# The last batch's late norm steps handed to the next stage, and two sets of semaphores, in a twelve-stage decoder kernel

## The reference

```python
x = _layernorm(x + _L0_attn_ref(x, ...), axis=-1)
x = _layernorm(x + _L0_xattn_ref(ctx_1024, x, ...), axis=-1)
x = _layernorm(x + _L0_ffn_ref(x, ...), axis=-1)
x = _layernorm(x + _L1_attn_ref(x, ...), axis=-1)
...
x = _layernorm(x + _L3_ffn_ref(x, ...), axis=-1)

def _layernorm(x, axis=-1, eps=1e-05):
    m = jnp.mean(x, axis=axis, keepdims=True)
    v = jnp.var(x, axis=axis, keepdims=True)
    return (x - m) / jnp.sqrt(v + eps)
```

## Time and profile before

| what | us |
|---|---|
| median of 3 runs (lowest, highest) | 3104.22 (3101.42, 3107.92) |
| the profiled execution | 3098.92 |
| its span | 3097.2 |

### The profile page before, as it was taken

How to read it: one execution, slowest core, us unless ns; L and a number is a source line. 1 busy time by engine, 2 the same in 40 slices (tenths; PEclk the granted TensorE clock), 3 DMA queues, 4 the chain that set the end, 5 groups by cost and what they waited for, 6 DMA issues and landing times. The chain is left out here.

```text
span 3097.2 us, 43720 instructions
## 1 busy us (share of the span) xinstructions
PE 2643.9 (85%) x15420; PEld 1245.2 (40%) x15420; DVE 2037.3 (66%) x5373; ACT 1334.3 (43%) x2298; POOL 996.5 (32%) x1254
## 2 busy tenths in 40 slices
PE   6997869988775988898988999988764999798998
PEld 1333324423322433454563444444332333344555
DVE  6885851269996746676784666657576887673444
ACT  2775642275642642221213433435641577463221
POOL 3212100078896101333443555563045111210000
PEclk9998979988977989999999999998875899899999
DMA  5322300000002500122230000003100321320000
GB/s 127 64 36 43 77 21 1 0 1 0 1 0 49 115 10 19 28 52 57 52 73 20 1 1 1 1 4 61 21 0 11 53 48 27 81 60 1 4 4 8
DMA packets 52134, 95.66 MB, mean 31 GB/s; under 512 B 14966, under 2 KB 36266, under 8 KB 46462
## 3 DMA queue, kind: packets, MB, share of 16 engines
q1 hardware_dynamic: 50620, 90.39, 13.9%
q10 hardware_dynamic: 1296, 2.47, 0.3%
HBM read 46.20 MB, written 1.38 MB: 15 GB/s over the span
## 5 line engine op out<-in xcount | busy, mean ns | idle before, releaser
L1970 POOL TENSOR_TENSOR mamba_dbu<-mamba_du,mamba_b 128x512 f32<-128x512 f32 x128 | 244.4, 1909 | 41.9 <-DVE stream L2003 12.1
L2003 DVE TENSOR_TENSOR_SCAN stream<-mamba_da,mamba_dbu 128x512 f32<-128x512 f32 x128 | 215.2, 1682 | 18.3 <-issue 13.1
L1714 PE MATMUL ps<-stream,weights 128*128 128x512 f32 x256 | 154.3, 714 | 57.8 <-DVE stream L2013 42.7
L2858 DVE CUSTOM_DVE_ANT_0 ps<-ps,bconst 128x512 f32<-128x512 f32 (+3 forms) x256 | 119.4, 512 | 116.0 <-PE ps L2685 116.0
L664 DVE TENSOR_REDUCE L3a_negmax<-ps 128x1 f32<-128x512 f32 x256 | 160.7, 683 | 25.2 <-PE ps L368 25.1
L664 DVE TENSOR_REDUCE L0a_negmax<-ps 128x1 f32<-128x512 f32 x256 | 160.6, 683 | 23.4 <-PE ps L368 23.3
L485 ACT ACTIVATE L0a_probs<-ps 128x512 f32<-128x512 f32 x256 | 141.7, 600 | 60.3 <-PE ps L387 59.4
L485 ACT ACTIVATE L3a_probs<-ps 128x512 f32<-128x512 f32 x256 | 141.9, 601 | 56.6 <-PE ps L387 55.7
L2921 ACT ACTIVATE skv_probs<-ps 128x1024 f32<-128x1024 f32 (+3 forms) x128 | 90.2, 704 | 175.5 <-PE ps L2710 175.5
L165 POOL TENSOR_SCALAR vareps<-mv 128x4 f32<-128x4 f32 x24 | 8.8, 367 | 487.5 <-DVE mv L1444 487.3
L190 PE MATMUL ps<-stream,xT 128*64 128x512 f32 x512 | 126.9, 612 | 14.4 <-DVE moa_v L2461 7.2
(11 more groups left out here) (668 smaller groups left out, 6499.3 us busy)
## 6 DMA issues: line engine op xcount, KB each, us to landing
moa_masks<-picked SPq DMA_DIRECT2D x32, 512.0 KB, 6.6
stream<-stream SPq DMA_DIRECT2D x28, 192.0 KB
stream<-gate_up_down_in SPq DMA_DIRECT2D x16, 272.0 KB, 3.4
stream<-value_output_in SPq DMA_DIRECT2D x16, 256.0 KB, 3.6
pre<-gates SPq DMA_DIRECT2D x32, 128.0 KB
stream<-ffn_in SPq DMA_DIRECT2D x16, 180.5 KB, 2.9
pre<-pre SPq DMA_DIRECT2D x40, 64.0 KB
L0a_qs<-L0a_qs SPq DMA_DIRECT2D x16, 128.0 KB
```

What stands on the lines that cost most here:

```text
L1714: pe.matmul(ps[:, SUM_BANK + j, :], k.ident, hc[:, (J * i + j) % RING, :], start=n == 0, stop=n == N - 1).then_inc(s["summed"], 1)
L1970: pool.tensor_tensor(dbu[:, m % RING, :], du[:, b % 2, j, :], bsb[:, i % B_RING, :], ALU.mult).then_inc(s["dbu_ready"], 1)
L2003: dve.tensor_tensor_scan(out=hs[:, m % RING, :], data0=da[:, m % RING, :], data1=dbu[:, m % RING, :], initial=0.0, op0=ALU.mult, op1=ALU.a ...
L2858: last = dve.tensor_tensor_reduce(ps[:, bank + a, 0:n], ps[:, bank + a, 0:n], later[:, SEQ - n:], -1.0, 3e38, ALU.add, ALU.min, negmax[:, ...
```

## The change

Two parts. First, `phase` draws from two pools of 50 semaphores in turn. The block's own barrier stays, SP's clearing comes behind it, and the second barrier is gone (also behind the last stage).

Second, in every stage but the last, batch 3's steps behind the statistics are left out (`left_over`), and each stage but the first does them for its forerunner, on six semaphores of their own (`k.late`) that count stages and are never cleared. POOL's two instructions (`late_deviation`) and DVE's four (`late_rescale`) stand at or near the head of their queues; PE's four turns (`late_turn`) and ACT's copy (`late_keep`) stand some steps later, in a PSUM bank that is free then; `late_known` is a wait ahead of the first reader. With mamba as the forerunner DVE rescales where ACT did, and POOL's two instructions for the offset (1975, 1976) fall away for batch 3. In the cross attentions the clearing of `v` moves to the very head of DVE's queue, ahead of `late_rescale`.

```diff
 def phase(k, *names):
...
-    assert len(names) <= len(k.pool), (len(names), len(k.pool))
-    s = dict(zip(names, k.pool))
+    pool = k.pools[k.stage % 2]
+    assert len(names) <= len(pool), (len(names), len(pool))
+    s = dict(zip(names, pool))
     with nc.Block() as block:
         yield block, s
-    used = k.pool[:len(names)]
-    nc.sync.sem_clear(range(used[0].num, used[-1].num + 1))
-    nc.all_engine_barrier()
+    nc.sync.sem_clear(range(pool[0].num, pool[len(names) - 1].num + 1))
+    k.stage += 1
...
+LATE = ("var", "eps", "rstd", "x", "xT", "sb")
+
+
+def left_over(k, b):
+    return b == BATCH - 1 and k.stage < STAGES - 1
+
+
+def late_deviation(k, pool):
+    if k.stage:
+        pool.wait_ge(k.late["var"], k.stage)
+        pool.tensor_scalar(k.vareps[:, :], k.mv[:, :, 1], EPS, None, ALU.add).then_inc(k.late["eps"], 1)
+        pool.wait_ge(k.late["eps"], k.stage)
+        pool.tensor_tensor(k.rstd[:, :], k.vareps[:, :], k.minus_half, ALU.pow).then_inc(k.late["rstd"], 1)
+        pool.wait_ge(k.late["rstd"], k.stage)
+
+
+def late_rescale(k, dve):
+    if k.stage:
+        dve.wait_ge(k.late["rstd"], k.stage)
+        for t in range(NT):
+            last = dve.tensor_scalar(k.xs[:, BATCH - 1, t, :], k.resid[:, t, :], k.mv[:, t, 0:1], k.rstd[:, t:t + 1],
+                                     ALU.subtract, ALU.mult)
+        last.then_inc(k.late["x"], 1)
+        dve.wait_ge(k.late["x"], k.stage)
+
+
+def late_turn(k, pe, bank):
+    if k.stage:
+        pe.wait_ge(k.late["x"], k.stage)
+        for t in range(NT):
+            last = pe.transpose(k.ps[:, bank, t * P:(t + 1) * P], k.xs[:, BATCH - 1, t, :], k.ident)
+        last.then_inc(k.late["xT"], 1)
+
+
+def late_keep(k, act, bank):
+    if k.stage:
+        act.wait_ge(k.late["xT"], k.stage)
+        act.copy(k.xTs[:, BATCH - 1, :], k.ps[:, bank, :]).then_inc(k.late["sb"], 1)
+
+
+def late_known(k, eng, sem="sb"):
+    if k.stage:
+        eng.wait_ge(k.late[sem], k.stage)
...
                 def turn_x(b):
+                    if left_over(k, b):
+                        return
                     pe.wait_ge(s["x_ready"], b + 1)
...
-                    last.then_inc(s["var_ready"], 1)
+                    last.then_inc(k.late["var"] if left_over(k, b) else s["var_ready"], 1)
...
+                    if J == LATE_AT:
+                        late_turn(k, pe, Z_BANK)
+                    if J == LATE_AT + 2:
+                        late_known(k, pe)
...
             @block.gpsimd
             def _(pool):
                 chain = Chain(pool, s["pool_chain"])
+                late_deviation(k, pool)
...
+                pad_v()
+                late_rescale(k, dve)
                 dec = out_t[:, :].rearrange("p (t d) -> p t d", t=NT)
...
                 for J in range(FIRST, LAST):
-                    if batch_at(J, PAD_AT) == 0:
-                        pad_v()
...
                 scale_logits(0)
+                late_rescale(k, dve)
                 route(0)
```

More of the change, by code:

```diff
@@ L28 @@
 PIECES = 16
+STAGES = 12
 SMALL = ["wq", "wk", "wv", "wo", "bv", "bo", "bq", "bk"]
@@ L760, in _ @@
                             add_out(batch_at(J, Y_AT + 1))
-                        if batch_at(J, Y_AT + 2) is not None and a == 1:
-                            b = batch_at(J, Y_AT + 2)
+                        b = batch_at(J, Y_AT + 2)
+                        if b is not None and a == 1 and not left_over(k, b):
                             scaled(k.xs[:, b], b + 1).then_inc(s["x_ready"], 1)
@@ L1171, in _ @@
                             rstd(2 * batch_at(J, Y_AT) + 1)
-                        if batch_at(J, Y_AT + 1) is not None:
-                            rstd(2 * batch_at(J, Y_AT + 1) + 2)
-                    elif batch_at(J, Y_AT + 1) is not None:
+                        b = batch_at(J, Y_AT + 1)
+                        if b is not None and not left_over(k, b):
+                            rstd(2 * b + 2)
+                    elif batch_at(J, Y_AT + 1) is not None and not left_over(k, batch_at(J, Y_AT + 1)):
                         rstd(batch_at(J, Y_AT + 1) + 1)
@@ L1258, in stats @@
                         last = dve.bn_aggr(k.mv[:, t, :], k.stats[:, t, :])
-                    last.then_inc(s["var_ready"], 1)
+                    return last
                 def scaled(out, n):
@@ L1279, in half_stats, with aggregate @@
                     chain(last)
-                def aggregate():
+                def aggregate(b):
                     for t in range(NT):
                         last = dve.bn_aggr(k.mv[:, t, :], k.stats[:, t, :])
-                    last.then_inc(s["var_ready"], 1)
+                    last.then_inc(k.late["var"] if left_over(k, b) else s["var_ready"], 1)
+                pad_v()
+                late_rescale(k, dve)
                 dec = out_t[:, :].rearrange("p (t d) -> p t d", t=NT)
@@ L1340, in _ @@
                             else:
-                                aggregate()
-                        if batch_at(J, XT_AT) is not None and a == 1:
-                            b = batch_at(J, XT_AT)
+                                aggregate(batch_at(J, Y_AT + 1))
+                        b = batch_at(J, XT_AT)
+                        if b is not None and a == 1 and not left_over(k, b):
                             scaled(k.xs[:, b], 2 * b + 2 if scrambled else b + 1).then_inc(s["x_ready"], 1)
@@ L1435, in residual, with statistics @@
         chain(ins)
-    statistics(k, dve, chain, s)
-def statistics(k, dve, chain, s):
+    statistics(k, dve, chain, s, b)
+def statistics(k, dve, chain, s, b):
     for t in range(NT):
@@ L3116, in _ @@
                         experts(batch(J, 1), 6, 8)
+                    if J == 0:
+                        late_turn(k, pe, D_BANK)
+                    if J == 2:
+                        late_known(k, pe)
                     if batch(J, 4) is not None:
@@ L3577, in build @@
         k.gates = nc.dram_tensor("gates", (BATCH, 8, SEQ), F32).ap()
-        k.pool = [ctx.enter_context(nc.semaphore(f"stage_{i}")) for i in range(50)]
+        k.pools = [[ctx.enter_context(nc.semaphore(f"{n}_{i}")) for i in range(50)] for n in ("even", "odd")]
+        k.late = {n: ctx.enter_context(nc.semaphore(f"late_{n}")) for n in LATE}
+        k.stage = 0
         def load(sp, g):
```

93 lines of the change are left out of this document (87 added, 6 removed).

## The result

| what | before | after |
|---|---|---|
| median of 4 runs (lowest, highest), us | 3104.57 (3101.42, 3107.92) | 3054.43 (3052.86, 3060.65) |
| the profiled execution, us | 3098.92 | 3052.86 |
| its span, us | 3097.2 | 3051.2 |
| busy PE, DVE, ACT, POOL, us | 2643.9, 2037.3, 1334.3, 996.5 | 2628.2, 2043.9, 1332.4, 1000.8 |
| mean granted TensorE clock | 0.924 | 0.934 |

The ratio of after to before is 0.9844, with a 95% interval of 0.9831 to 0.9856: 50 us, or 1.6%, faster. The forecast was 3059 us in a range of 3047 to 3072. No engine's work changed by more than four small instructions (PE's busy time fell since its clock was at half for a shorter time, and 47 of its 15420 matmul records are missing in this profile), so the time went where nothing overlapped.

What follows compares the result with a forecast made beforehand. Bound taken: batch 3's serial late steps and barriers at eleven joints, 58.0 us without overlap. 48.8 + 0.3 - 3.2 + 2.2 - 4.1 - 0.65 - 0.5 + 2.3 = 45.2 us off 3098.9 gives 3053.7, plus 5.3: median 3059, range 3047 to 3072.

Steps and rivals of the forecast that it cites:

- The joints: Eleven joints between stages shrink to 0.3 us each, except where SP holds L2a's and mamba's: 48.8 us gained.
- rival D: At the joints the chain only moves and only the second barrier's time is gained, about 4 us: 3100 us, chance 0.04.
- L0x and L2x: At these heads the rescale, stretched by POOL's clearing, starts the value bias 1.6 us late, twice: 3.2 us lost.
- rival C: POOL's clearing locks out the rescale in L0x, L2x and L3x for longer: 3066 to 3072 us, chance 0.2.
- L1x and L3x: Clearing v before the mask arrives starts the value bias 1.35 us earlier in L1x, 0.8 in L3x: 2.2 us gained.
- the mask arrives at S+6.4: In L1x the mask comes 6.4 us after the stage's start S, so the value bias starts at S+8.35.
- PE's turns: PE's four moved turns cost 1.1 us in L2a, 0.5 or 0.3 in eight other stages: 4.1 us lost.
- First DVE work of moa and L3f: DVE's first work waits behind the rescale at both heads: 0.5 us lost in moa, 0.65 in L3f.
- the route: In L3f route starts 0.9 us late behind the rescale, delaying rffn_hid, so PE loses 0.65 us.
- the clock's 3.0 in L3f: PE's shorter rest before L3f avoids the half-clock stretch at its head, returning 3.0 us if full clock is kept.
- The clock, +2.3: Shorter PE rests at the joints before mamba and L3f keep full clock: 2.3 us gained, between 0 and 4.7.
- a stage more than 4 us longer: Sign of a wrong prediction: any stage longer by more than 4 us from its start to its last mv.

Runs made afterwards that it cites:

- Run 1: Kernel before with only the two alternating semaphore sets, so no second barrier, batch 3's late steps left in place: 3100.6 us, ratio 0.9991.
- run 2: Changed kernel with one semaphore set and the second barrier put back, late steps still moved into the next stage: 3057.68 us, ratio 0.9853.
- Run 3: Changed kernel, but in the cross attentions POOL waits for the rescale's end before clearing qs and ks: 3050.77 us in a single run.
- run 5: Changed kernel, but in the four cross attentions DVE's rescale stands behind batch 0's value bias: 3055.24 us, ratio 0.9854.
- run 7: Changed kernel, but SP issues the six DMAs turning L1x's and L2x's ahead copies at those stages' heads: 3050.74 us in a single run.
- run 6: Changed kernel unaltered, measured and profiled again: 3056.26 us, ratio 0.9848; its line relates L2a's length to time at 0.50 across six profiles.
- Run 9: Changed kernel with PE's turn in L2a, DVE's rescale and PE's turn in moa, and the rescale in L3f placed elsewhere: 3047.47 us, ratio 0.9824.
- run 8: Changed kernel, but POOL's two clearings for the ahead copies stand at the heads of mamba and L2a: 3049.05 us in a single run.

## Why the prediction was right, step by step

**The joints.** 48.8 forecast, 49.0 measured. The barrier that stays is 0.3 us and what is behind SP's last DMA is 0.87, with 0.9 assumed. Run 1 and run 2 show that the two barriers' half and the chain's half are independent; rival D, by which the chain only moves, is out, since run 2 alone brings 45 us.

**L0x and L2x.** The step held in every row: rescale 1.56 and 1.59 us against a forecast of 1.6, bias at S+4.12 and S+4.14 against S+4.15. Run 3 shows the cause that was only inferred from the earlier trace rows: without POOL's clearing beside it the rescale takes 1.11. That the clearings take turns with the rescale's instructions, and do not shut it out until they are all done, decided against rival C. Wherever a clearing met the rescale, two of its four instructions ended behind one clearing. The Trainium skill, page "SBUF — State Buffer", section "Who interferes with whom", has DVE and GpSimd lock each other out for whole instructions; the rows agree with that (a 1.80 us clearing became 1.95, the rescale 1.56, 2.28, 2.67, or 3.86 in L3a, where two long clearings stand beside it), but not with the reading that every single instruction of the rescale would lose. What the stages then took was less than forecast, +0.8 in L2x and -0.2 in L0x instead of +1.9: in L0x PE stays 1.5 behind until S+145 and is then ahead, with 10 us less at 0.50; in L2x the 1.6 of the head are 1.4 at S+25 and 0.8 from S+96 on. In run 5, when the head is faster, a part of the gain goes the same way. SP's queue comes last behind the head in run 7; whether POOL's does was not tested.

**L1x and L3x.** L3x came as forecast: bias at S+6.09 against S+6.05, PE 0.8 earlier. For L1x I forecast the bias at S+8.35 and found S+6.09, 2.3 us better. The step that failed is "the mask arrives at S+6.4": I took for a property of the code what differs from one execution to the next. `mask_q` in the two profiles of the same changed kernel, with the POOL clearing that it meets:

```profile
962.86 1.51 DVE L1316 TENSOR_SCALAR L1x_mask_q<-L1x_raw_q 128x616 bf16<-128x616 int32 x1 [0.57 <-DMA L1x_raw_k<-mask_kq]
964.30 0.47 DVE L1304 TENSOR_TENSOR L1x_v<-ps,weights 77x128 f32<-77x128 f32 x2
```
```profile
962.09 1.95 POOL L1203 MEMSET L1x_qs<- 64x2048 f32 x1
```
```profile
965.95 2.10 DVE L1316 TENSOR_SCALAR L1x_mask_q<-L1x_raw_q 128x616 bf16<-128x616 int32 x1 [2.28 <-DMA L1x_raw_k<-mask_kq]
967.97 0.47 DVE L1304 TENSOR_TENSOR L1x_v<-ps,weights 77x128 f32<-77x128 f32 x2
```
```profile
965.91 1.80 POOL L1203 MEMSET L1x_qs<- 64x2048 f32 x1
```

The first starts at S+4.65, in the middle of a clearing, and ends 0.34 us behind that clearing's end, at 964.38. The second starts at S+6.37, ends 0.34 behind the next long one, and its bias is at S+8.39, which is my figure. In the DMA records the last packet of the mask's second transfer ends at S+3.6 in the first profile and S+5.2 in the second, and at S+5.0 in the profile of before. Over all twelve profiles, whatever the kernel, `mask_q` of L1x starts between S+4.65 and S+6.46: before's S+6.46 is the latest of them. So the bias of L1x came 3.6 us earlier than before in the first profile and 1.3 in the second. The head of before with an early mask (run 1, `mask_q` at S+4.76) has its bias at S+9.16, 3.1 behind the first profile, so the new order is worth as much only when the mask is early.

**PE's turns.** In L2a +1.1 forecast; the turn stands without a gap between its neighbours, and before's code lay 0.8 to 1.0 below the line of run 6:

```profile
1608.47 1.98 PE L191 MATMUL ps<-weights,xT 128*64 128x512 f32 x4 [0.93 <-DVE skv_kT L2984]
1610.38 1.12 PE L225 MATMUL ps<-weights,x_tok 128*128 128x128 f32 x4
1610.49 0.59 ACT L3051 COPY stream<-ps 128x512 f32<-128x512 f32 x1 [4.98 <-PE ps L191]
1611.42 1.23 PE L2798 MATMUL ps<-skv_kT,skv_qT 64*128 64x512 f32 x2
```

Run 9 takes it back by putting the turn into the 0.93 us that PE waits in the first of these rows. In L3f the turn cost 0.46 and in mamba 0.6, against 0.5. What the turns cost in the four cross attentions and L3a was not separated.

**First DVE work of moa and L3f.** Moa was priced at 0.5 and the first work came 0.65 later. For L3f I had 0.65 for the route; DVE and PE there after the change:

```profile
2767.44 1.11 DVE L215 TENSOR_SCALAR x_tok<-resid,mv,rstd 128x128 f32<-128x128 f32 x4
...
2772.61 1.29 DVE L3642 TENSOR_TENSOR rffn_hid<-rffn_sg,ps 128x512 f32<-128x512 f32 x2
```
```profile
2771.29 1.02 PE L3542 MATMUL ps<-xT,stream 128*128 128x512 f32 x2
2773.36 1.10 PE L3541 MATMUL ps<-xT,stream 128*96 128x512 f32 x2 [1.04 <-DVE rffn_hid L3642]
```

`rffn_hid` starts 0.2 us later against the stage's start than before in this profile and 0.8 later in the second (forecast 0.9). PE waits 1.04 us for it, because PE came there early: its clock had risen 4.2 us behind the start, not 6.1. The wait took back exactly that lead, so two of my terms, the route and the clock's 3.0 in L3f, were not independent. Counting both was wrong: with DVE's chain ending at about S+7.3, no clock could give back more than 0.1 there.

**The clock, +2.3.** This is the term that failed. What it named did not happen where it was named: mamba's fall came all the same (0.50 from S+0.7 to S+4.1), and L3f gave nothing. What did happen was not in it: L2f gained 1.55 at its head, where the clock rose at S+5.5 instead of S+10.8 (not in the second profile); moa lost 1.4 at its head, at 0.50 until S+11.5 instead of S+7.7; and moa and L3f had three new stretches of 3.4 us at 0.50, 1.7 us each, all behind rests of PE (2.5 us in L3f, 3.3 in moa) that the profile of before has too, there without a fall. Over all stages the profile of the change is 3.5 us longer where I had 3.95, but that nearness is luck: single stages miss by up to 4.5 us (L3f, +4.17 for -0.35), and the second profile is 7.8 us longer than before in its stages. The Trainium skill, page "TensorE: Matmul & The Clock Gate", section "What's actually happening", says that the clock is lost through idleness and regained through work. These stretches behind rests agree with it, and the same rests without a fall show that it does not say when; a joint of 0.3 us without PE did not keep it in these rows, since PE still rests 2.38 us there, the time from its own last work of the stage.

I said that a stage more than 4 us longer would show me wrong. L3f is, by 4.17. The rows of the two stretches and run 1 say that most of it is the clock; the moved steps hold 0.46 of it, in the second profile 1.05 of 4.72.

## What to carry to other kernels

Work at the end of a stage that only the next stage reads belongs behind the barrier, and there behind the first work that another engine waits for, if it stands in a wait at its new place too (L0x, L2x, L2a and L3f gained so, moa and L3x did not). Before a wait is removed, look at who else the barrier waits for: here SP's last DMAs kept 5.5 of 58 us, and moving those DMAs into the next stage only pushed its own ones back, while an earlier start of the chain that feeds them gained 3.7. Edits that gain alone can meet each other: the clearing of run 8 stands beside the rescale of L2a and took back what run 9 had gained there. When a term of under 5 us is to be read from one profile, read the time at half clock of each stage first: it moved single stages of one and the same code by up to 6.5 us.

## What the runs showed of the hardware

- A `tensor_scalar` of DVE that starts beside a POOL clearing ends a fixed time behind that clearing, so its price is quantized: `mask_q` of L1x started during a clearing in all twelve profiles, at any point of it, took 0.50 to 2.15 us, and ended 0.34 us behind a clearing's end every time. Four rescales took 1.11, 1.29, 1.56, 2.28, 2.67, 2.94 or 3.86 us by their place. A mask 1.7 us later made the stage's bias 2.3 later. The value bias, a `tensor_tensor` from PSUM, took its 0.48 us beside a clearing as without one.
- What the clearing lengthens in the timeline is the duration of the DVE instruction, not the wait ahead of it: the start of `mask_q` follows the mask's last DMA packet by 0.8 to 1.5 us in all twelve profiles, wherever POOL is in its clearing.
- Behind one and the same rest of PE the granted clock sometimes falls and sometimes stays. PE rests 2.51 to 2.53 us for `rffn_hid` at three places of L3f in all twelve profiles. In 17 of these 36 cases the clock went to 0.50 within 1.5 us of the rest's end, for 3.4 us each time, and a stretch cost 1.5 to 1.7 us; in the other 19, the three of before among them, it stayed at 1.00. What decides was not found; it was not tried with a delay put in on purpose.
- The time at 0.50 in moa, L2a and L3f changed from kernel to kernel with no edit in the stage (L2a 3.4 to 20.2 us).
- At equal time at 0.50, L2a's length in six profiles of the same code lay within 0.14 us of a line, which is a way to see an edit of 1 us.
